# A four-layer model (two scans, two attention and feed-forward layers): TensorE gets zero-weight matmuls, VectorE takes three steps of the last feed-forward stages

## The chip, the cores and the metric

The kernel runs on one core of one Trainium2 chip. The metric is the device time of one execution in microseconds; the median of three runs before the change is 11572.21 us.

## What is computed

The input x is 4 images of 64 x 64 pixels with 96 channels, float32. Four layers follow each other, each with a residual:

```python
# layer 0 and 1: group norm, then a selective scan in four directions (K = 4, 192 channels, 16 states)
xz = x @ in_proj_w.T;  xi, z = split(xz)
xc = silu(depthwise_conv3x3(xi) + conv_b)
xs = four orders of the 4096 pixels of xc
dts, Bs, Cs = split(einsum('bkdl,kcd->bkcl', xs, x_proj_w))
delta = softplus(einsum(dts, dt_w) + dt_b)
h = exp(dt_t * A) * h + (dt_t * u_t) * B_t       # for each pixel t
y = einsum('bkdn,bkn->bkd', h, C_t)
y = layer_norm(sum of the four y + Ds * xs) * silu(z);  x = x + y @ out_proj_w.T
# layer 2 and 3: attention without softmax, then a feed-forward part in 8-bit floats
t = t + attn(layer_norm(t));  t = t + ffn(layer_norm(t))
# ffn: q_mul rounds to e5m2, q_acc to 5 exponent and 10 mantissa bits
h = relu(q_acc(q_acc(q_mul(x) @ q_mul(W1).T) + q_mul(b1)))
y = q_acc(q_acc(q_mul(h) @ q_mul(W2).T) + q_mul(b2))
```

## The kernel before

**Scan phase.** Eight scans (4 images x 2 layers) are run one after another. Each has 16 windows (4 directions x 4 blocks of T = 1024 pixels), so W = 128 windows, and a window has NT = 24 tiles of 128 partitions x 1024 elements: 3072 tiles, numbered n, with i = n % 24. Three groups of GT = 8 tiles make a window. For each tile:
- TensorE broadcasts B into one of two PSUM slots with two bf16 matmuls (`fill`, L1019), after VectorE's scan has released the slot (tile n's after the scan of tile n - 2);
- VectorE multiplies the slot by delta times u (`inp`, L1538) and runs the recurrence (`states`, L1553 and L1549), with the decay that ScalarE has made with an exponential (L1288);
- GpSimd multiplies the states by C (`product`, L1632), and TensorE adds up the states of two tiles in the bank YB with four matmuls in four column strips (`reduce2`, L1032, issued at even i for tiles n - 4 and n - 3). The sum over a group of eight tiles is open from i % 8 = 4 to the reduce2 at i % 8 = 2 of the next group; ScalarE then collects it from YB (L1303).

The last two tiles of a group (`on_pool`) have no fill: ScalarE writes their decay into the slot, and GpSimd makes their input (L1646).

**Side jobs.** Beside the tiles each engine steps through the same list of jobs, two ticks per tile, in an order that the program fixes: "pre" (group norm, and the convolution as nine fp32 matmuls per half and chunk, L826, and L830), "post" (y is loaded and summed with fp32 matmuls, L861, then layer norm L872, L873, L880, projection L887), and "attn" (attention L914 to L952, then the feed-forward part). Per scan there are one pre, one post and, for each image pair, attention jobs. In between TensorE prepares the next windows (L994, L1000, L1010). On every engine instructions run in the order of the program text; a wait holds up all that stands behind it on that engine.

**After the last scan** the jobs of the last window list run alone (`overlapped` is False): post of scan 7 and attn 6 and 7. Chunks of 512 pixels go through three lanes of buffers, FF_LANES = 6 ticks apart. In the feed-forward part chunk c is, at s = tick - 6c: centred on TensorE (s = 0, L961); copied and squared on ScalarE (1, L1204, L1205); its variance on TensorE (2, L965); logarithm and exponential on ScalarE (3, L1208, L1210); scaled and cast by VectorE to `xq` (5, L1527); w1 on TensorE in three parts (6 to 8, L973), each rounded to f16 by ScalarE (7 to 9, L1214); then `s == 10` on ScalarE: three rectifiers with bias (L1218) and the cast to fp8 (L1222); w2 on TensorE (12, L980); rounding (L1226) and bias (L1228) on ScalarE (13); addition to the image on GpSimd (15, L1613). The same functions, with `overlapped` True, serve the feed-forward parts beside the scans, 12 ticks apart and with one lane. Semaphores `fh_a`, `fc_a` and `fb_a` count rectifiers, casts and biases.

Of the kernel before, what the change touches and what calls it, by code (L numbers as in the profile page):

```python
# [13 lines left out]
CH = 96  # L14
# [184 lines left out]
SUMS = (1, 3, 0, 2, K)  # L199
SUM_AT = (0, 2, 4, 8, 10)  # L200
A1_EVERY, A2_EVERY, FF_EVERY = 9, 1, 12
LANES = 3
POST_LANES, A1_LANES, FF_LANES = 13, 4, 6

# [34 lines left out]
def build_program(nc, a, out):  # L239
# [17 lines left out]
    with ctx:  # L257
# [52 lines left out]

        selb = sb("selb", [CH, NQ, 128], BF16)
        neg = sb("neg", [CH, 2, CH], BF16)
        red = sb("red", [128, DB])
        eye = sb("eye", [CH, CH])
        cen = sb("cen", [CH, CH])
# [78 lines left out]
        def rows(v):  # L394
# [51 lines left out]
        mid_p, mid_v = sem("mid_p"), sem("mid_v")  # L446
        ao_p, ao_v = sem("ao_p"), sem("ao_v")
        fc_p, fs_a, fv_p, fr_a, fq_v = sem("fc_p"), sem("fs_a"), sem("fv_p"), sem("fr_a"), sem("fq_v")
        f1_p, f1_a, fh_a, fc_a, f2_p, fy_a, fb_a, fx_g = (sem("f1_p"), sem("f1_a"), sem("fh_a"), sem("fc_a"),
                                                         sem("f2_p"), sem("fy_a"), sem("fb_a"), sem("fx_g"))  # L450
        o_out = sem("o_out")

        after_wait_p, after_wait_v, after_wait_a = sem("after_wait_p"), sem("after_wait_v"), sem("after_wait_a")
# [331 lines left out]
        def _(pe):  # L785
# [106 lines left out]
            def attn(N, overlapped):  # L892
# [61 lines left out]
                for tick in range(ff_ticks(overlapped)):  # L954
                    for c in range(C8):
                        s, m = tick - ff_every(overlapped) * c, M + c
                        v = lane(c, overlapped)
                        if s == 0:
                            pe.wait_ge(ao_v, M + C8)
                            after(pe, f1_a, HT * through(m, c, overlapped))  # L960
                            pe.matmul(ps[0:CH, v.bank, :], cen96[:, :], chunk(c), start=True, stop=True).then_inc(fc_p, 1)  # L961
                        if s == 2:
                            pe.wait_ge(fs_a, m + 1)
                            after(pe, fy_a, through(m, c, overlapped))
                            pe.matmul(ps[0:CH, v.bank + 1, :], o96[:, :], v.sq, start=True, stop=True).then_inc(fv_p, 1)  # L965
                        if s in (6, 7, 8):
                            r = s - 6
                            if r == 0:
                                pe.wait_ge(fq_v, m + 1)
                            if r == 2:  # L970
                                pe.wait_ge(f1_a, HT * m + 1)
                            pe.sem_inc(after_wait_p, 1)
                            pe.matmul(ps[:, v.bank + r % 2, :], w1q[:, l, r * 128:(r + 1) * 128], v.xq,  # L973
                                      start=True, stop=True).then_inc(f1_p, 1)
                        if s == 12:
                            pe.wait_ge(fc_a, m + 1)
                            pe.wait_ge(f1_a, HT * m + 2)
                            pe.sem_inc(after_wait_p, 1)
                            for r in range(HT):
                                mm = pe.matmul(ps[0:CH, v.bank + 1, :], w2q[:, l, r, :], v.hq[:, r, :],  # L980
                                               start=(r == 0), stop=(r == HT - 1))
                            mm.then_inc(f2_p, 1)
                    yield

            stages = {"pre": pre, "post": post, "attn": attn}


            def x_dbl(hf, w):
                s, k = w // STEPS, w % STEPS // NCH
# [23 lines left out]
            def fill(n):  # L1013
                w, i = divmod(n, NT)
                if i == 0:
                    pe.wait_ge(s_a, 6 * w + 6)
                after(pe, scan_v, n - RS + 1)
                for hf in range(2):
                    mm = pe.matmul(ps[:, SLOT + 2 * (n % RS) + hf, :], selb[:, i % GT // 2, :],  # L1019
                                   sbc[:, w % 2, B * hf:B * (hf + 1)], start=True, stop=True)  # L1020
                mm.then_inc(fill_p, 1)

            def reduce2(m):
# [40 lines left out]
            for w in range(W):  # L1064
                if w % STEPS == 0:
                    side = beside(plan[w // STEPS + 1], stages, True)
                    if w == 0:
                        side = follow(head, side)
                if w % STEPS == STEPS - 1:
                    run(side)  # L1070
                for i in range(NT):
                    n = w * NT + i
                    if n + 1 < W * NT and not on_pool(n + 1):
                        fill(n + 1)
                    if i % 2 == 0 and n >= 4:
                        reduce2((n - 4) // 2)
                    for tick in (2 * i, 2 * i + 1):
                        prepare_at(tick, w + 1)
                        prepare_at(tick - 2 * NT, w + 2)
                        next(side, None)  # L1080
            for m in range(W * NP - 2, W * NP):
                reduce2(m)
            run(beside(plan[NSC + 1], stages, False))
# [3 lines left out]
        def _(act):  # L1087
# [78 lines left out]
            def attn(N, overlapped):  # L1166
# [29 lines left out]
                for tick in range(ff_ticks(overlapped)):  # L1196
                    for c in range(C8):
# [13 lines left out]
                        if s in (7, 8, 9):  # L1211
                            r = s - 7
                            act.wait_ge(f1_p, HT * m + r + 1)
                            act.activation(v.h16[:, r, :], ps[:, v.bank + r % 2, :], ACT.Identity).then_inc(f1_a, 1)  # L1214
                        if s == 10:
                            for r in range(HT):
                                act.wait_ge(f1_a, HT * m + r + 1)
                                act.activation(v.h16[:, r, :], v.h16[:, r, :], ACT.Relu, bias=b1q[:, l, r:r + 1]).then_inc(fh_a, 1)  # L1218
                            act.wait_ge(fh_a, HT * (m + 1))
                            after(act, f2_p, through(m, c, overlapped))  # L1220
                            act.sem_inc(after_wait_a, 1)
                            act.activation(v.hq, v.h16, ACT.Identity, saturate=False).then_inc(fc_a, 1)  # L1222
                        if s == 13:
                            act.wait_ge(f2_p, m + 1)
                            after(act, fx_g, through(m, c, overlapped))
                            act.activation(v.y16, ps[0:CH, v.bank + 1, :], ACT.Identity).then_inc(fy_a, 1)  # L1226
                            act.wait_ge(fy_a, m + 1)
                            act.activation(v.y16, v.y16, ACT.Identity, bias=b2q[:, l:l + 1]).then_inc(fb_a, 1)  # L1228
                    yield

            stages = {"pre": pre, "post": post, "attn": attn}
# [139 lines left out]
        def _(dve):  # L1371
# [99 lines left out]
            def attn(N, overlapped):  # L1471
# [47 lines left out]
                for tick in range(ff_ticks(overlapped)):  # L1519
                    for c in range(C8):  # L1520
                        s, m = tick - ff_every(overlapped) * c, M + c
                        v = lane(c, overlapped)
                        if s == 5:
                            dve.wait_ge(fr_a, 2 * m + 2)
                            after(dve, f1_p, HT * through(m, c, overlapped))
                            dve.sem_inc(after_wait_v, 1)
                            dve.tensor_tensor(v.xq, v.xa, ps[0:CH, v.bank + 1, :], ALU.mult, saturate=False).then_inc(fq_v, 1)  # L1527
                    yield

            stages = {"pre": pre, "post": post, "attn": attn}  # L1530
# [45 lines left out]
        def _(pool):  # L1576
            pool.memset(xb[:, :, :], 0.0).then_inc(set_g, 1)
            pool.memset(eps[:, :], 1e-5)
            pool.memset(zero[:, :], 0.0).then_inc(set_g, 1)
            pool.wait_ge(set_v, SET_V)  # L1580

# [19 lines left out]
            def attn(N, overlapped):  # L1601
# [7 lines left out]
                for tick in range(ff_ticks(overlapped)):  # L1609
                    for c in range(C8):  # L1610
                        if tick - ff_every(overlapped) * c == 15:
                            pool.wait_ge(fb_a, M + c + 1)
                            pool.tensor_tensor(chunk(c), chunk(c), rows(lane(c, overlapped).y16), ALU.add).then_inc(fx_g, 1)  # L1613
                    yield

# [137 lines left out]
```

## Time and profile before

| | |
|---|---|
| median of three runs | 11572.21 us (11567.04 to 11578.72) |
| profiled execution | 11564.55 us |
| its span, first to last instruction | 11562.8 us |
| mean granted TensorE clock | 0.741 |
| busy: VectorE, GpSimd, TensorE, ScalarE | 10132.7, 9737.8, 8819.7, 7059.3 us |

All times are microseconds on the one core. PE is TensorE, PEld its weight loads, DVE VectorE, ACT ScalarE, POOL GpSimd. A granted clock of 1.00 is 2.4 GHz, 0.50 is 1.2 GHz; a mean between them is a mixture of the two in time. A group's row gives the count and total busy time, the mean ns of one, then the idle time of the engine just before them and what ended it. A timeline row gives start, duration, engine, line, operation and count of merged instructions, and in brackets the idle time before. An fp32 matmul appears as two records.

### The profile page before, as it was taken

How to read it: one execution, taken by the hardware profiler on the slowest of the kernel's cores; microseconds unless marked ns; L12 is line 12 of the kernel's file. 1: busy time of each engine (PE TensorE's matmuls, PEld its weight loads, DVE VectorE, ACT ScalarE, POOL GpSimd, SP SyncE). 2: the span in 40 equal slices, each digit the busy share in tenths (PEclk: the TensorE clock that was granted, in tenths of full speed). 3: DMA queues.
4: the chain of work that ended last, by engine and by line, in shares of the span. 5: the costliest groups of instructions: out<-in, count | busy, mean ns of one | idle time of the engine just before them, and what ended most of it. 6: DMA issues, size and time to landing. Idle time of an engine off the chain costs nothing.

```text
span 11562.8 us, 94504 instructions
## 1 busy us (share of the span) xinstructions
PE 8819.7 (76%) x26272; PEld 2210.7 (19%) x26272; DVE 10132.7 (88%) x6006; ACT 7059.3 (61%) x10794; POOL 9737.8 (84%) x4231
## 2 busy tenths in 40 slices
PE   6876678876879677769777787787787977777756
PEld 2211111211112111212112121122111221121212
DVE  3899998999889998989989999899989999898871
ACT  4665555665556555667555765566655666567646
POOL 3899988899888998989988888888888889898850
PEclk8875577875779667769777787788677976777766
DMA  3666689566775556656766668957677656565540
GB/s 100 143 139 132 142 150 162 143 138 142 159 160 144 139 145 156 153 130 147 166 150 152 133 141 171 157 133 154 130 159 161 144 133 159 151 149 126 130 118 6
DMA packets 1781802, 1631.74 MB, mean 141 GB/s; under 512 B 1323982, under 2 KB 1325296, under 8 KB 1781276
## 3 DMA queue, kind: packets, MB, share of 16 engines
q1 hardware_dynamic: 1781276, 1625.69, 63.7%
q8 instruction: 212, 3.47, 0.1%
q14 instruction: 314, 2.57, 0.1%
HBM read 625.58 MB, written 194.51 MB: 71 GB/s over the span
## 4 chain that ended last, share of the span: by engine, by line
DVE 16%; PE 16%; issue 15%; POOL 12%; ACT 7%; DMA 3%; SPq 3%; DVEq 0%; POOLq 0%; ACTq 0%
POOL pr L1632 8%; DVE hs L1553 7%; DVE ps L1538 6%; DVE hs L1549 3%; PE ps L1032 3%; PE ps L861 2%; PE ps L1019 2%; PE ps L826 1%; PE ps L1010 1%; ACT dec L1288 1%; POOL bup L1646 1%; POOL dur L1646 1%; PE ps L994 1%; POOL us L1623 1%; SPq L720 1%
## 5 line engine op out<-in xcount | busy, mean ns | idle before, releaser
L1632 POOL TENSOR_TENSOR pr<-hs,crep 128x1024 f32<-128x1024 f32 x3072 | 7183.5, 2354 | 1194.5 <-PE ps L1032 571.8
L1553 DVE TENSOR_TENSOR_SCAN hs<-dec,carry,ps 128x1024 f32<-128x1024 f32 x1728 | 4054.7, 2346 | 240.4 <-POOL pr L1632 14.0
L1538 DVE TENSOR_TENSOR ps<-ps,dur 128x1024 f32<-128x1024 f32 x2304 | 2790.1, 1211 | 513.9 <-PE ps L1019 372.5
L1019 PE MATMUL ps<-sbc,selb 96*128 96x512 bf16 x4608 | 1844.5, 493 | 1789.8 <-DVE hs L1553 1248.3
L1288 ACT ACTIVATE dec<-dtr,ac 128x1024 f32<-128x1024 f32 x2304 | 2610.9, 1136 | 436.4 <-DVE hs L1553 427.7
L1032 PE MATMUL ps<-pr,red 128*32 128x512 f32 x12288 | 2285.0, 827 | 33.0 <-POOL pr L1632 24.5
L1295 ACT ACTIVATE carry<-hs 128x1 f32<-128x1 f32 x2304 | 456.9, 199 | 2434.7 <-DVE hs L1553 2265.4
L1553 DVE TENSOR_TENSOR_SCAN hs<-dec,zero,ps 128x1024 f32<-128x1024 f32 x576 | 1351.5, 2346 | 86.0 <-ACT dec L1288 14.1
L826 PE MATMUL ps<-xb,tapw 96*96 96x512 f32 x2304 | 1187.2, 637 | 55.9 <-ACT sd L1122 53.4
L1019 PEld LDWEIGHTS ps<-sbc,selb 96*128 96x128 bf16 x4608 | 382.5, 108 | 3922.6 <-DVE hs L1553 2313.5
L1288 ACT ACTIVATE ps<-dtr,ac 128x1024 f32<-128x1024 f32 x768 | 848.4, 1105 | 400.0 <-DVE hs L1553 399.8
L1646 POOL TENSOR_TENSOR dur<-dur,brep 128x1024 f32<-128x1024 f32 x384 | 907.1, 2362 | 46.2 <-DVE ps L1538 46.1
L1646 POOL TENSOR_TENSOR bup<-dur,brep 128x1024 f32<-128x1024 f32 x384 | 905.0, 2357 | 27.3 <-DMA brep<-bc_d 27.3
L1010 PE MATMUL ps<-xdf,tapw 6*96 6x512 f32 x1024 | 781.0, 852 | 45.7 <-ACT de L1263 29.1
L994 PE MATMUL ps<-us,xp 96*102 96x512 f32 x1024 | 685.7, 806 | 78.9 <-ACT us L1241 59.5
L1623 POOL TENSOR_TENSOR us<-us,de 96x1024 f32<-96x1024 f32 x256 | 602.4, 2353 | 157.1 <-ACT de L1272 157.1
L861 PE MATMUL ps<-sd,eye 96*96 96x512 f32 x896 | 644.1, 840 | 105.1 <-DMA sd<-y_d 102.1
L1549 DVE TENSOR_TENSOR_SCAN hs<-ps,carry,bup 128x1024 f32<-128x1024 f32 x288 | 671.3, 2331 | 57.9 <-ACT ps L1288 44.1
L1549 DVE TENSOR_TENSOR_SCAN hs<-ps,carry,dur 128x1024 f32<-128x1024 f32 x288 | 670.4, 2328 | 17.7 <-POOL dur L1646 9.5
L826 PEld LDWEIGHTS ps<-xb,tapw 96*96 96x96 f32 x2304 | 359.4, 170 | 775.3 <-issue 680.1
L1032 PEld LDWEIGHTS ps<-pr,red 128*32 128x32 f32 x12288 | 276.5, 124 | 1175.8 <-issue 887.5
L1255 ACT ACTIVATE sbc<-ps 96x512 bf16<-96x512 f32 x768 | 444.0, 578 | 25.9 <-PE ps L1000 25.6
(224 smaller groups left out, 7595.9 us busy)
## 6 DMA issues: line engine op xcount, KB each, us to landing
dtr<-de SPq DMA_DIRECT2D x768, 512.0 KB, 8.0
dur<-us SPq DMA_DIRECT2D x768, 512.0 KB, 8.6
crep<-bc_d SPq DMA_DIRECT2D x512, 512.0 KB, 6.6
ust<-u_d SPq DMA_DIRECT2D x256, 384.0 KB, 5.9
y_d<-yst SPq DMA_DIRECT2D x768, 128.0 KB, 3.3
sd<-y_d SPq DMA_DIRECT2D x448, 192.0 KB, 5.1
brep<-bc_d SPq DMA_DIRECT2D x128, 512.0 KB, 5.6
u_d<-sd SPq DMA_DIRECT2D x64, 384.0 KB, 3.2
```

The lines of the kernel that those rows point to most:

```text
L826: mm = pe.matmul(bank, tap[:, t, h * CH:(h + 1) * CH], xb[:, c * ROWS + t // 3:c * ROWS + t // 3 + ROWS, t % 3:t % 3 + SIDE], start=(t == ...
L861: mm = pe.matmul(ps[0:CH, bank + h, :], eye[:, :] if k < K else dg[:, l, h, :], v, start=(i == 0), stop=(i == K))
L994: mm = pe.matmul(ps[0:XROWS, PB, :], xp[:, l, h, k, :], us[:, half(h, w), B * hf:B * (hf + 1)], start=(h == 0), stop=(h == 1))
L1010: pe.matmul(ps[0:CH, PB, :], dtw[:, order[s][1], k, h * CH:(h + 1) * CH], xdf[XD:XROWS, :], start=True, stop=True, tile_position=(XD, 0)). ...
L1019: mm = pe.matmul(ps[:, SLOT + 2 * (n % RS) + hf, :], selb[:, i % GT // 2, :], sbc[:, w % 2, B * hf:B * (hf + 1)], start=True, stop=True)
L1032: mm = pe.matmul(ps[32 * strip:32 * strip + 32, YB, :], red[:, :], pr[:, (2 * m + j) % RP, B * hf:B * (hf + 1)], start=(q == 0), stop=(q = ...
L1288: act.activation(to, dtr[:, 2 * (G % 2) + i % 2, :], ACT.Exp, scale=ac[:, order[s][1], k, i:i + 1]).then_inc(exp_a, 1)
L1538: dve.tensor_tensor(slot(n), slot(n), dur[:, 2 * (G % 2) + i % 2, :], ALU.mult).then_inc(bu_v, 1)
L1549: dve.tensor_tensor_scan(hs[:, n % RH, :], slot(n), bup[:, :] if i % 2 else dur[:, 2 * (G % 2), :], init, ALU.mult, ALU.add).then_inc(scan ...
L1553: dve.tensor_tensor_scan(hs[:, n % RH, :], dec[:, others(n) % RD, :], slot(n), init, ALU.mult, ALU.add).then_inc(scan_v, 1)
L1632: pool.tensor_tensor(pr[:, n % RP, :], hs[:, n % RH, :], crep[:, q, :], ALU.mult).then_inc(prod_g, 1)
L1646: pool.tensor_tensor(to, v, brep[:, :], ALU.mult).then_inc(bup_g, 1)
```

## The change

First, in the scan phase, `keep_busy()` issues BUSY = 3 matmuls at the end of tile i on TensorE, for the tiles in which the sum in YB is open (i % 8 not 2 or 3). Their weights are `nil`, 96 x 128 zeros in bf16, their moving data 512 columns of `selb`, and they add zero to YB. In the tiles after i % 8 = 2 and 3 the two fill matmuls are issued twice instead. Second, in the feed-forward parts after the last scan, VectorE does the three rectifiers (s = 8, 9, 10), the cast (11) and the second bias (14) instead of ScalarE. Semaphores are renamed; the feed-forward parts beside the scans stay on ScalarE.

```diff
@@ TensorE
+            def open_sum(i):
+                return i % GT not in (2, 3)
+            def keep_busy():
+                for _ in range(BUSY):
+                    pe.matmul(ps[:, YB, :], nil[:, :], selb[:, :, :].rearrange("p q n -> p (q n)"),
+                              start=False, stop=False, skip_group_check=True)
@@ fill(n)
-                for hf in range(2):
-                    mm = pe.matmul(ps[:, SLOT + 2 * (n % RS) + hf, :], selb[:, i % GT // 2, :],
-                                   sbc[:, w % 2, B * hf:B * (hf + 1)], start=True, stop=True)
+                for again in range(1 if open_sum(i - 1) else 2):
+                    for hf in range(2):
+                        mm = pe.matmul(ps[:, SLOT + 2 * (n % RS) + hf, :], selb[:, i % GT // 2, :],
+                                       sbc[:, w % 2, B * hf:B * (hf + 1)], start=True, stop=True)
                 mm.then_inc(fill_p, 1)
@@ end of a tile on TensorE
                         next(side, None)
+                    if n >= 4 and open_sum(i):
+                        keep_busy()
@@ ScalarE, feed-forward
-                        if s == 10:
+                        if overlapped and s == 10:
...
                             act.activation(v.y16, ps[0:CH, v.bank + 1, :], ACT.Identity).then_inc(fy_a, 1)
-                            act.wait_ge(fy_a, m + 1)
-                            act.activation(v.y16, v.y16, ACT.Identity, bias=b2q[:, l:l + 1]).then_inc(fb_a, 1)
+                            if overlapped:
+                                act.wait_ge(fy_a, m + 1)
+                                act.activation(v.y16, v.y16, ACT.Identity, bias=b2q[:, l:l + 1]).then_inc(f_bias, 1)
@@ VectorE, feed-forward
+                        if not overlapped and s in (8, 9, 10):
+                            r = s - 8
+                            dve.wait_ge(f1_a, HT * m + r + 1)
+                            dve.tensor_scalar(v.h16[:, r, :], v.h16[:, r, :], b1q[:, l, r:r + 1], 0.0,
+                                              ALU.add, ALU.max).then_inc(f_relu, 1)
+                        if not overlapped and s == 11:
+                            dve.wait_ge(f_relu, HT * (m + 1))
+                            after(dve, f2_p, through(m, c, overlapped))
+                            dve.tensor_copy(v.hq, v.h16, saturate=False).then_inc(f_cast, 1)
+                        if not overlapped and s == 14:
+                            dve.wait_ge(fy_a, m + 1)
+                            dve.tensor_scalar(v.y16, v.y16, b2q[:, l:l + 1], None, ALU.add).then_inc(f_bias, 1)
@@ GpSimd, at the start
+            pool.memset(nil[:, :], 0.0)
```

## Rows read from the trace of the kernel before

**Rows 1.** The page: busy time of the engines, and TensorE's clock in 40 slices.

```profile
PE 8819.7 (76%) x26272; PEld 2210.7 (19%) x26272; DVE 10132.7 (88%) x6006; ACT 7059.3 (61%) x10794; POOL 9737.8 (84%) x4231
...
PEclk8875577875779667769777787788677976777766
```

**Rows 2.** Windows, busy us and instructions by engine, then clock, DMA, GB/s.

```profile
800.00:1400.00 600.00, 406.80 (x1164) 69.34 (x1164) 581.58 (x322) 333.10 (x483) 566.89 (x246) 0.57 0.62 130
...
652.16:678.12 25.96, 24.59 (x86) 7.66 (x84) 25.00 (x15) 18.79 (x30) 22.68 (x11) 1.00 0.54 124
...
sum 2070.00, PE 1882.49 PEld 547.00 DVE 1898.62 ACT 1450.84 POOL 1836.21; mean PE 268.93 PEld 78.14 DVE 271.23 ACT 207.26 POOL 262.32
...
1500.00:2100.00 600.00, 482.71 (x1337) 109.27 (x1336) 537.95 (x314) 344.30 (x507) 527.32 (x228) 0.75 0.85 157
...
sum 4070.00, PE 3220.07 PEld 747.89 DVE 3687.45 ACT 2364.44 POOL 3613.69; mean PE 460.01 PEld 106.84 DVE 526.78 ACT 337.78 POOL 516.24
...
11460.00:11560.00 100.00, 49.88 (x89) 14.00 (x88) 9.39 (x14) 67.45 (x104) 8.91 (x8) 0.61 0.07 14
```

**Rows 3.** Timeline of VectorE, no side job: start us, us, what.

```profile
811.53 1.21 DVE L1538 TENSOR_TENSOR ps<-ps,dur 128x1024 f32<-128x1024 f32 x1
...
837.64 1.21 DVE L1538 TENSOR_TENSOR ps<-ps,dur 128x1024 f32<-128x1024 f32 x1
```

**Rows 4.** Timeline of TensorE beside the convolution, 650 to 700.

```profile
652.16 0.59 PE L1019 MATMUL ps<-sbc,selb 96*128 96x512 bf16 x2
652.59 1.88 PE L994 MATMUL ps<-us,xp 96*102 96x512 f32 x4
```

**Rows 5.** Waits of VectorE in the whole span: total, times, longest.

```profile
DVE ps L1538 <- PE ps L1019: 372.5, 241, 7.3
```

**Rows 6.** Windows around three waits of VectorE for the fill.

```profile
410.54:413.85 3.31, 3.27 (x5) 0.60 (x3) 2.87 (x2) 2.01 (x4) 2.05 (x2) 0.50 0.28 64
...
1834.50:1844.83 10.33, 8.48 (x20) 2.36 (x21) 3.00 (x2) 3.23 (x5) 7.66 (x5) 0.60 1.02 286
...
11023.33:11028.50 5.17, 4.05 (x12) 1.41 (x15) 2.86 (x2) 4.24 (x7) 1.97 (x1) 0.54 0.01 3
```

**Rows 7.** Timeline of the longest of them, in the first post.

```profile
1836.35 3.73 PE L861 MATMUL ps<-sd,eye 96*96 96x512 f32 x4 [5.66 <-DMA sd<-y_d]
...
1844.83 1.23 DVE L1538 TENSOR_TENSOR ps<-ps,dur 128x1024 f32<-128x1024 f32 x1 [7.34 <-PE ps L1019]
```

**Rows 8.** Timeline of the last two feed-forward stages.

```profile
11358.53 0.72 ACT L1228 ACTIVATE crep<-crep,b2q 96x512 f16<-96x512 f16 x1
...
11363.22 0.66 ACT L1208 ACTIVATE ps<-ps,eps 96x512 f32<-96x512 f32 x1 [1.14 <-PE ps L965]
...
11364.40 1.93 ACT L1218 ACTIVATE sd<-sd,b1q 128x512 f16<-128x512 f16 x3
...
11364.66 0.68 DVE L1527 TENSOR_TENSOR pr<-pr,ps 96x512 fp8e5<-96x512 f32 x1 [11.04 <-ACT ps L1210]
...
11366.47 1.48 ACT L1222 ACTIVATE sd<-sd 128x1536 fp8e5<-128x1536 f16 x1
...
11369.38 0.63 PE L973 MATMUL ps<-pr,w1q 96*128 96x512 fp8e5 x1
11369.80 1.92 PE L961 MATMUL ps<-xb,cen 96*96 96x512 f32 x2
...
11372.89 2.02 PE L965 MATMUL ps<-crep,o 96*96 96x512 f32 x2 [0.31 <-ACT crep L1205]
...
11479.99 1.48 PE L980 MATMUL ps<-sd,w2q 128*96 128x512 fp8e5 x3 [4.92 <-ACT sd L1222]
...
11555.78 1.48 PE L980 MATMUL ps<-pr,w2q 128*96 128x512 fp8e5 x3 [4.23 <-ACT pr L1222]
```

**Rows 9.** Groups of VectorE in the first 60 us, casts to fp8.

```profile
L1376 DVE CAST w1q<-dur 96x768 fp8e5<-96x768 f32 x1 | 0.5, 549 | 0.0
L1377 DVE CAST w2q<-dur 128x576 fp8e5<-128x576 f32 x1 | 0.4, 449 | 0.0
```

More of the change, by code:

```diff
@@ L201 @@
 A1_EVERY, A2_EVERY, FF_EVERY = 9, 1, 12
+BUSY = 3
 LANES = 3
@@ L312, in build_program @@
         neg = sb("neg", [CH, 2, CH], BF16)
+        nil = sb("nil", [CH, 128], BF16)
         red = sb("red", [128, DB])
@@ L448, in build_program @@
         fc_p, fs_a, fv_p, fr_a, fq_v = sem("fc_p"), sem("fs_a"), sem("fv_p"), sem("fr_a"), sem("fq_v")
-        f1_p, f1_a, fh_a, fc_a, f2_p, fy_a, fb_a, fx_g = (sem("f1_p"), sem("f1_a"), sem("fh_a"), sem("fc_a"),
-                                                         sem("f2_p"), sem("fy_a"), sem("fb_a"), sem("fx_g"))
+        f1_p, f1_a, f_relu, f_cast, f2_p, fy_a, f_bias, fx_g = (sem("f1_p"), sem("f1_a"), sem("f_relu"), sem("f_cast"),
+                                                               sem("f2_p"), sem("fy_a"), sem("f_bias"), sem("fx_g"))
         o_out = sem("o_out")
@@ L975, in attn @@
                         if s == 12:
-                            pe.wait_ge(fc_a, m + 1)
+                            pe.wait_ge(f_cast, m + 1)
                             pe.wait_ge(f1_a, HT * m + 2)
@@ L1214, in attn @@
                             act.activation(v.h16[:, r, :], ps[:, v.bank + r % 2, :], ACT.Identity).then_inc(f1_a, 1)
-                        if s == 10:
+                        if overlapped and s == 10:
                             for r in range(HT):
                                 act.wait_ge(f1_a, HT * m + r + 1)
-                                act.activation(v.h16[:, r, :], v.h16[:, r, :], ACT.Relu, bias=b1q[:, l, r:r + 1]).then_inc(fh_a, 1)
-                            act.wait_ge(fh_a, HT * (m + 1))
+                                act.activation(v.h16[:, r, :], v.h16[:, r, :], ACT.Relu, bias=b1q[:, l, r:r + 1]).then_inc(f_relu, 1)
+                            act.wait_ge(f_relu, HT * (m + 1))
                             after(act, f2_p, through(m, c, overlapped))
                             act.sem_inc(after_wait_a, 1)
-                            act.activation(v.hq, v.h16, ACT.Identity, saturate=False).then_inc(fc_a, 1)
+                            act.activation(v.hq, v.h16, ACT.Identity, saturate=False).then_inc(f_cast, 1)
                         if s == 13:
@@ L1611, in attn @@
                         if tick - ff_every(overlapped) * c == 15:
[L1612 removed]
+                            pool.wait_ge(f_bias, M + c + 1)
                             pool.tensor_tensor(chunk(c), chunk(c), rows(lane(c, overlapped).y16), ALU.add).then_inc(fx_g, 1)
```

## The prediction

> **What bounds the kernel now.** I read the page's busy shares first, then the windows stage by stage, then the waits of VectorE, and last the timelines of the two places that the change touches. Over the whole span VectorE is the busiest engine at 88%, GpSimd has 84% and TensorE 76%, and TensorE's granted clock is a mixture of its two levels: the slices of PEclk run from 5 to 8 tenths [rows 1]. The windows show why [rows 2]. The scan phase goes through 3072 tiles with side jobs beside them.
> - With no side job (800 to 1400) VectorE is busy for 581.58 of 600 us, or 97%. Records of neighbours touch there, so 97% is its ceiling. Eight tiles go from 811.53 to 837.64 [rows 3], 26.11 us, or 3.264 us a tile. TensorE is busy 68% at clock 0.57, mostly on its level of 1.2 GHz, and nobody waits for it.
> - Beside the convolution of "pre" (seven stretches, 2070 us together) VectorE falls to 1898.62/2070 = 91.7% and TensorE is at 91%, with a clock of 1.00 in eight tiles without a disturbance (652.16 to 678.12). A tile takes 3.264 x 0.969/0.917 = 3.45 us, which makes 600 tiles.
> - Beside "post" (seven stretches, 4070 us) VectorE has 90.6%, TensorE 79%; the first stretch, 1500 to 2100, has clock 0.75.
> - After the last scan, in the two feed-forward stages, VectorE does next to nothing (9.39 of 100 us), ScalarE is busy for 67% and TensorE for half, at clock 0.61.
>
> What VectorE waits for in the scan phase is above all the broadcast of B, L1019: 372.5 us in 241 waits [rows 5]. I looked at the granted clock in the 3 us before each of these waits and during it: of the 223 waits over 0.3 us (369 us), 151 with 279 us stand at a mean clock under 0.75; the first and the last of them are [rows 6]. So up to 279 us of the scan phase go with a slow TensorE clock.
>
> **Part 1, the zero-weight matmuls.** In six of eight tiles TensorE gets 3 more 512-column bf16 matmuls, and in the other two the 2 fill matmuls are issued twice: 18 + 4 = 22 in eight tiles, 8448 in all. The matmuls go into bank YB; the sums of L1032 there and ScalarE's collecting keep their order, so no engine but TensorE gets a wait from them. Their price is the spacing of such matmuls in a full queue. At clock 1.00 the two fills of 652.16 are followed by the next group at 652.59 [rows 4]: 0.215 us each. At the low level the w1 matmul of 11369.38 is followed by the next group at 11369.80 [rows 8], 0.42 us; I take twice 0.215, 0.43 us each. So 22 cost 4.73 us per eight tiles at the high level, 0.59 us a tile, and 1.18 us at the low one.
>
> Beside the convolution this lands on an engine that is full. The eight tiles from 652.16 to 678.12 take 25.96 us with TensorE busy for 24.59 [rows 2] at clock 1.00. With 4.73 more it needs 29.32 us, more than VectorE's 26.11: TensorE becomes the bound there, at 3.665 us a tile. Against 3.45 now that is +0.215 us on 600 tiles, **+129 us**. The low end is 3.55 us a tile, if the records' gaps between short matmuls absorb part of the addition (+60 us); the high end is 3.80, if waits of the kind seen today (TensorE 91% busy, not 100%) stay on top (+210 us). I take the middle, since a queue that never runs dry has few of them.
>
> Of the Trainium skill one rule bears on that price. Its page "TensorE: Matmul & The Clock Gate", section "Back-to-back issue gap", gives some 131 ns per matmul for a sustained stream of weight loads and 512-column matmuls. By that figure eight tiles would take 24.59 + 2.9 = 27.5 us, 3.44 a tile, and the term would be an estimated 0 in place of the cost above. The trace's 0.215 us [rows 4] disagrees and is used.
>
> Everywhere else the added matmuls lie in time in which TensorE waits. With no side job VectorE has 2.35 us of scan and 1.21 us of multiply between the release of a slot and the need for the next fill, and the fill itself needs 0.43 to 1.0; 3 zero matmuls (0.65 to 1.3 us) fit. There they bring nothing either, as VectorE is at its ceiling. I put 0 on these 2100 us, with +20 as the bad end, since at the low level TensorE would need about 68% of 3.264 plus 1.18, 3.4 us a tile, until the clock rises.
>
> What comes back is a part of the 279 us. It can't be all. The program order of TensorE is fixed: a zero matmul that stands behind a blocked instruction runs after it, not instead of the idle time. The worst wait shows it [rows 7]: TensorE sits idle for 5.66 us on a load of y, then works off its backlog, and VectorE gets its fill 7.34 us late at 1844.83. The first rows of that backlog run at the low level (four passes in 3.73 us, against 1.88 for four passes in [rows 4]). Nothing in the change fills those 5.66 us; it adds two sets of three matmuls, 1.3 to 2.6 us, to the backlog. The smaller waits, which come after ordinary idle time between fills, should shrink by half or more. I take 45% of 279, **-126 us**, between 5% (-15) and 85% (-240). Attention, whose matmuls wait for ScalarE and VectorE step by step, gives perhaps 12 us more, **-12 us** (0 to -40).
>
> What I leave aside is the idle time itself: the window around that wait has clock 0.60 [rows 6], it begins with the late load, and no added matmul makes the load come sooner.
>
> **Part 2, the last two feed-forward stages.** There a chunk goes round a loop in which ScalarE has everything. The w2 matmuls of neighbouring chunks start at 11479.99 and, seven chunks on, at 11555.78: 10.83 us a period [rows 8]. In a period ScalarE does the evacuations, logarithm and exponential (11363.22), three rectifiers (11364.40, 1.93 us), the cast (11366.47, 1.48 us), only then w2 starts (it waits for L1222 as in the row of 11555.78), and the y16 bias follows (11358.53, 0.72 us). The change takes 1.93 + 1.48 + 0.72 us from ScalarE. VectorE then has, per chunk, three 128x512 f16 ops, a cast of 1536 columns and a 512-column add. Neither exists in the trace. Bounds from casts [rows 9]: 768 columns took 0.549 us and 576 took 0.449, so 0.52 ns a column, and 1536 columns take 0.95 us; 512 take 0.42. The other end is one column in 1.04 ns: 1.75 and 0.68 (the 512-column op of L1527 has 0.68, [rows 8]). In all 2.6 to 4.5 us a period, beside ScalarE, so VectorE doesn't become the bound.
>
> What is late next is the normalisation loop: w1 of chunk D at 11369.38, centring of E, its squares, o96 at 11372.89 for 2.02 us, 0.03 to the logarithm: 5.56 us; then from the logarithm at 11363.22 to the end of xq at 11364.66 + 0.68: 2.12 us; then w1 of E. That is 7.7 us at the low level [rows 8]. The matmuls in it shorten at the high level by up to 1.9 us, so 5.8 to 7.7. The clock was 0.61 there [rows 2], so I take 7.4. Fourteen periods save 14 x (10.83 - 7.4) = 48 us, and the last chunk of each stage has a shorter way to its end: 3.41 us of rectifiers and cast become 0.42 + 0.95, and the bias saves 0.3, some 2.3 us, twice. Together **-53 us** (-40 if VectorE runs at one column per 1.04 ns, with its cast in the loop; -75 if the clock rises). The wait order is safe: on VectorE only the xq of the next chunk is queued behind the cast, and it needs the exponential, which ends later than the cast. GpSimd's adds wait for the bias as before and have slack.
>
> **The sum.** +129 - 126 - 12 - 53 = -62 us against the profiled execution's 11564.55 us; the median of the runs, 11572.21, lies 7.7 above it. So 11564.6 - 62 + 7.7 = **11510 us**.
>
> **The rivals.**
> - *A: the clock stays up nearly everywhere.* Six zero matmuls in a pause keep TensorE at 2.4 GHz between fills, the small waits go, attention follows: -240 - 40 in the scan phase, +110 beside the convolution, -75 at the end, in sum -245, so 11327; halfway to the forecast it gives 11410. For it: where TensorE's queue is full, its clock is 1.00 [rows 2]. Against: [rows 7], and that TensorE at the high level with the added work is busy for under two thirds of a stretch with no side job. Chance 0.18, time about 11400.
> - *E: a full queue takes the added matmuls for less than their spacing*, since weight loads and short records overlap. Then eight tiles beside the convolution stay within today's 3.45 us a tile, the +129 falls away and 11381 is left. Against it: the 0.215 us of [rows 4] are read in just such a full queue. The Trainium skill's figure above is the reason to list it. Chance 0.05.
> - *B: the convolution loses more than the rest gives.* One mechanism: beside "pre" TensorE is already full, and 22 more matmuls per eight tiles are paid in full, at 3.80 us a tile (+210), while only 15% of the waits come back (-42) and the end gives -50. Sum +118, so 11690. It decides against the change from the point where the scan phase loses over 76 us, since the end gives 53 and 23 is the measurable bound. For it: 24.59 of 25.96 us busy. Chance 0.20, times from 11595 to 11700.
> - *C: both halves cancel.* The scan phase loses 30 to 76 us and the end gives it back. Chance 0.14, 11549 to 11595.
> - *D: the change does not do what it says*: the clock stays near 0.57 beside nothing and the added matmuls run at 0.43 us. Then the stretches without side jobs slow from 3.264 to 3.4 us a tile, 4% of 2100 us, +84 us on top of B. It is part of B's chance, 0.03 of it.
>
> **How the numbers follow.** Forecast (11450 to 11549) 0.43, A 0.18, E 0.05, C 0.14, B with D 0.20. A measurement can tell about 0.2%, 23 us, from no change. Faster: 0.43 + 0.18 + 0.05 = 0.66; same 0.14; slower 0.20. For eight in ten I leave out the far half of A and the far half of B: 11370 to 11625.
>
> **What would show it.** In the changed profile: the PEclk slices up from 5 to 8 tenths; beside the convolution TensorE at 97% or more and VectorE at 86 to 89%, a tile at 3.6 to 3.7 us; beside "post" VectorE at 92 to 93%; waits for L1019's successor beside "post" (now most of 372.5 us) down by half with the ones behind y loads still there; with no side job 97% as now. In the end the w2 matmuls 7.0 to 7.8 us apart and ScalarE waiting between. The forecast is wrong if the added matmuls cost much less than 0.215 us each in a full queue, if the clock beside "post" stays at 0.75, or if the loop at the end is set by VectorE's cast.

## The result: 1.6% slower

| | before | after |
|---|---|---|
| median | 11574.33 us | 11752.85 us (11744.01 to 11767.27) |
| ratio | | 1.0157, 95% interval 1.0142 to 1.0173 |
| span of the profiled execution | 11562.8 us | 11749.7 us |
| from the start of the first scan to that of the last | 10942.7 us | 11174.4 us |
| from there to the end | 430.4 us | 385.4 us |
| mean granted clock | 0.741 | 0.852 |

The clock rose as the change meant it to, the end became 45 us shorter, and the scan phase became 232 us longer. The page of the changed kernel, to be read against [rows 1]:

```profile
PE 9950.4 (85%) x34714; PEld 2931.7 (25%) x34714; DVE 10189.4 (87%) x6086; ACT 7003.7 (60%) x10714; POOL 9746.2 (83%) x4232
PEclk8887788887889778879888898899888988888876
```

TensorE went from 76% to 85% busy and its slices from 5 to 8 tenths up to 6 to 9. VectorE has the same scans and multiplies as before in a longer span. I numbered the scans in both traces (3072 of them) and compared equal pieces of work. The windows below hold the convolution's matmuls of seven scans (first sum), and the sums over y of seven posts (second sum). The same pieces before took 1919 us with TensorE busy for 1778 and VectorE for 1752 (clock 0.93 to 0.96), and 3620 us with 2902 and 3252 (clock 0.75 to 0.78). The last row is 600 us with no side job, to be read against the first of [rows 2].

```profile
2184.00:2474.00 290.00, 286.17 (x1037) 95.23 (x1036) 252.72 (x139) 184.65 (x261) 242.93 (x105) 0.99 0.60 138
sum 2036.00, PE 2011.43 PEld 668.71 DVE 1773.64 ACT 1332.31 POOL 1707.87; mean PE 287.35 PEld 95.53 DVE 253.38 ACT 190.33 POOL 243.98
...
1559.00:2100.00 541.00, 481.04 (x1563) 131.84 (x1562) 467.36 (x272) 300.09 (x437) 458.61 (x198) 0.85 0.86 159
sum 3682.00, PE 3250.41 PEld 913.01 DVE 3264.17 ACT 2091.31 POOL 3205.09; mean PE 464.35 PEld 130.43 DVE 466.31 ACT 298.76 POOL 457.87
...
800.00:1400.00 600.00, 457.56 (x1674) 109.05 (x1672) 580.92 (x323) 329.85 (x479) 567.49 (x245) 0.79 0.64 138
```

- Beside the convolution TensorE is now busy for 286.17 of 290 us at clock 0.99, and for 2011.43 of 2036 us, or 99%, in the seven windows together (before: 1778 of 1919, or 93%). It is the bound: +117 us for the same work.
- Beside post the clock went from 0.75 to 0.85, and the same work takes 62 us more, not less.
- With no side job VectorE has 580.92 us where it had 581.58, at clock 0.79 in place of 0.57. That higher clock bought nothing there. A VectorE scan takes 2346 ns in both traces, so VectorE's own work did not get slower; it waits more.

By groups of eight tiles, each put down to the side job that has matmuls in it, the 232 us are: beside the convolution +123 (3.494 to 3.691 us a tile), post +51, feed-forward +26, attention +5, none of these +27.

The waits grew where TensorE is waited for. The first row answers [rows 5] (372.5 us in 241 waits); GpSimd's wait for a free product buffer had 571.8 us before.

```profile
DVE ps L1568 <- PE ps L1034: 569.8, 384, 9.7
...
POOL pr L1663 <- PE ps L1047: 829.9, 384, 8.6
```

Sorted by the mean granted clock of each wait and the 3 us before it (waits over 0.3 us), as in the prediction:

| mean clock | before | after |
|---|---|---|
| under 0.75 | 279 us in 151 | 262 us in 111 |
| 0.75 to 0.95 | 63 us in 41 | 82 us in 30 |
| 0.95 and over | 27 us in 31 | 201 us in 136 |

The waits with a slow clock are nearly all still there, and a new class stands beside them: waits at a full clock, for a TensorE with too much in its queue.

The traces also show what TensorE did before each of these waits ended. I added up its records between the release of the slot (the end of the scan two tiles before) and VectorE's late start. In the changed kernel, zero-weight matmuls stand there in 249 of the 277 waits (491 of 545 us) and take 288 us of TensorE's time. In the waits with a clock under 0.75, TensorE's idle time fell from 123 us before to 67 after, but zero-weight matmuls take 133 us in its place. Most of the increase is at one place: VectorE's waits for the first tile of a group went from 177 to 320 us, all others together from 192 to 225.

At the end, the loop of the feed-forward stages, timeline rows that answer [rows 8], and a window over the second stage:

```profile
11582.19 0.96 DVE L1554 CAST crep<-crep 128x1536 fp8e5<-128x1536 f16 x1
...
11585.45 0.35 DVE L1557 TENSOR_SCALAR crep<-crep,b2q 96x512 f16<-96x512 f16 x1 [0.42 <-ACT crep L1243]
...
11583.30 1.48 PE L982 MATMUL ps<-crep,w2q 128*96 128x512 fp8e5 x3 [0.43 <-DVE crep L1554]
11585.17 0.59 PE L975 MATMUL ps<-sd,w1q 96*128 96x512 fp8e5 x1 [0.39 <-DVE sd L1545]
...
11588.63 2.02 PE L967 MATMUL ps<-pr,o 96*96 96x512 f32 x2 [0.31 <-ACT pr L1222]
11591.08 1.49 PE L982 MATMUL ps<-sd,w2q 128*96 128x512 fp8e5 x3 [0.43 <-DVE sd L1554]
...
11688.00:11744.00 56.00, 45.88 (x71) 12.09 (x71) 25.48 (x45) 31.26 (x56) 7.80 (x7) 0.50 0.12 25
```

The cast takes 0.96 us on VectorE and the bias 0.35; w2 starts every 7.78 us in place of 10.83. TensorE is busy for 45.88 of 56 us in that stage and its clock is 0.50 throughout; it idles 0.43, 0.39 and 0.31 us in a period.

### The profile page after: what moved, and what is told of

Same layout as the page of the kernel before. It is cut to its first block, busy times and chain, and to the rows that moved or that the text cites. A ratio compares the mean times of both kernels' runs of the same rounds, so it can differ in the third digit from the quotient of the medians.

```text
span 11749.7 us, 111386 instructions
## 1 busy us (share of the span) xinstructions
PE 9950.4 (85%) x34714; PEld 2931.7 (25%) x34714; DVE 10189.4 (87%) x6086; ACT 7003.7 (60%) x10714; POOL 9746.2 (83%) x4232
## 4 chain that ended last, share of the span: by engine, by line
PE 37%; issue 18%; DVE 17%; POOL 15%; ACT 7%; DMA 3%; SPq 3%; DVEq 0%; POOLq 0%; ACTq 0%
POOL pr L1663 10%; PE ps L828 7%; DVE hs L1583 7%; DVE ps L1568 6%; PE ps L1047 6%; PE ps L999 5%; PE ps L1034 5%; PE ps L863 3%; DVE hs L1579 3%; PE ps L1024 3%; PE ps L1008 2%; POOL bup L1677 1%; POOL us L1654 1%; ACT dec L1306 1%; POOL dur L1677 1%
## 5 line engine op out<-in xcount | busy, mean ns | idle before, releaser
L1663 POOL TENSOR_TENSOR pr<-hs,crep 128x1024 f32<-128x1024 f32 x3072 | 7193.5, 2356 | 1428.6 <-PE ps L1047 829.9
L1583 DVE TENSOR_TENSOR_SCAN hs<-dec,carry,ps 128x1024 f32<-128x1024 f32 x1728 | 4054.2, 2346 | 234.9 <-POOL pr L1663 10.4
L1568 DVE TENSOR_TENSOR ps<-ps,dur 128x1024 f32<-128x1024 f32 x2304 | 2792.8, 1212 | 707.9 <-PE ps L1034 569.8
L1034 PE MATMUL ps<-sbc,selb 96*128 96x512 bf16 x6144 | 1989.9, 432 | 1146.1 <-DVE hs L1583 918.0
L999 PE MATMUL ps<-selb,nil 96*128 96x512 bf16 x6906 | 2148.0, 426 | 0.0
L1047 PE MATMUL ps<-pr,red 128*32 128x512 f32 x12288 | 1994.4, 727 | 13.8 <-POOL pr L1663 11.5
L1583 DVE TENSOR_TENSOR_SCAN hs<-dec,zero,ps 128x1024 f32<-128x1024 f32 x576 | 1351.3, 2346 | 83.8 <-ACT dec L1306 12.8
L1034 PEld LDWEIGHTS ps<-sbc,selb 96*128 96x128 bf16 x6144 | 564.7, 105 | 2547.2 <-DVE hs L1583 1500.4
L999 PEld LDWEIGHTS ps<-selb,nil 96*128 96x128 bf16 x6906 | 671.1, 106 | 2063.1 <-issue 1783.1
L828 PE MATMUL ps<-xb,tapw 96*96 96x512 f32 x2304 | 1136.5, 613 | 20.3 <-ACT sd L1139 17.9
L1024 PE MATMUL ps<-xdf,tapw 6*96 6x512 f32 x1024 | 659.1, 727 | 34.9 <-ACT sbc L1273 20.6
L863 PE MATMUL ps<-sd,eye 96*96 96x512 f32 x896 | 597.9, 785 | 62.4 <-DMA sd<-y_d 60.1
L1008 PE MATMUL ps<-us,xp 96*102 96x512 f32 x1024 | 595.3, 712 | 57.9 <-ACT us L1259 48.5
```

The source lines that it names most:

```text
L828: mm = pe.matmul(bank, tap[:, t, h * CH:(h + 1) * CH], xb[:, c * ROWS + t // 3:c * ROWS + t // 3 + ROWS, t % 3:t % 3 + SIDE], start=(t == ...
L863: mm = pe.matmul(ps[0:CH, bank + h, :], eye[:, :] if k < K else dg[:, l, h, :], v, start=(i == 0), stop=(i == K))
L999: pe.matmul(ps[:, YB, :], nil[:, :], selb[:, :, :].rearrange("p q n -> p (q n)"), start=False, stop=False, skip_group_check=True)
L1024: pe.matmul(ps[0:CH, PB, :], dtw[:, order[s][1], k, h * CH:(h + 1) * CH], xdf[XD:XROWS, :], start=True, stop=True, tile_position=(XD, 0)). ...
L1047: mm = pe.matmul(ps[32 * strip:32 * strip + 32, YB, :], red[:, :], pr[:, (2 * m + j) % RP, B * hf:B * (hf + 1)], start=(q == 0), stop=(q = ...
L1568: dve.tensor_tensor(slot(n), slot(n), dur[:, 2 * (G % 2) + i % 2, :], ALU.mult).then_inc(bu_v, 1)
```

## The experiments

All of these kernels keep VectorE's share at the end. "Scan" is the difference in the time from the first to the last scan in one profiled execution, "end" that of the time behind it. One profile of a kernel lies up to 30 us beside its median (e3; 17 us in e5, under 12 in the others), so the difference of medians (each against the kernel before in the same session) is given too; less the -57.5 us of e1 it is a second estimate of the scan phase's part. The expectations below were written with slightly other spans (10932 us before, +235 after, +99 in e4); counted from the first to the last scan these are 10942.7, +232 and +102.

| run | added matmuls | median | scan | end | clock |
|---|---|---|---|---|---|
| after | 22 in 8 tiles | +178.5 | +232 | -45 | 0.852 |
| e1_tail_only | none | -57.5 | -4 | -51 | 0.741 |
| e2_zero_no_refill | 18 | +146.4 | +191 | -44 | 0.830 |
| e3_refill_only | 4 | -66.1 | +16 | -43 | 0.769 |
| e4_not_beside_pre | 22, not beside pre | +46.9 | +102 | -45 | 0.838 |
| e5_short | 18 of 64 columns, not beside pre | -27.4 | +35 | -46 | 0.746 |
| e6_six | 36, not beside pre | +242.1 | +288 | -53 | 0.875 |
| e7_gap | 18 in two tiles, not beside pre | +357.7 | +418 | -56 | 0.797 |
| e9_not_before_first_fill | 15, not beside pre | +48.0 | +88 | -43 | 0.807 |
| e10_only_before_first_fill | 3, not beside pre | -23.8 | +43 | -52 | 0.749 |
| e8_tail_zero | none in the scans, 3 a chunk at the end | -68.1 | -3 | -66 | 0.743 |
| e11_tail_zero_two | the same, 6 a chunk | -69.5 | +5 | -71 | 0.745 |

**The two halves apart.** Edit of e1_tail_only, relative to the changed kernel (e2 and e3 have one of the two hunks each):

```diff
-                for again in range(1 if open_sum(i - 1) else 2):
+                for again in range(1):
...
-                    if n >= 4 and open_sum(i):
-                        keep_busy()
```

> Only VectorE's share in the last two feed-forward stages; no zero-weight matmuls and no second fills. My theory (the end gives some 45 us, the scan phase is where all of the loss lies, and beside the convolution it is TensorE's queue): scan phase as before, 10932 us from the first to the last scan, the part after it 385 us in place of 430, total 11520 to 11530, ratio 0.996. Rival (the tail gains less, because something of the scan phase lends it a warmer clock): the part after the last scan stays over 400 us, total over 11535.

Measured: 11517.78 us, ratio 0.9957 (0.9942 to 0.9971). The scan phase is back at 10939 us, the end is 51 us shorter (379 us, under the 385 expected). So all of the loss is in the added matmuls, and VectorE's share alone is a gain.

> The changed kernel with its three zero-weight matmuls, but each fill issued once. Theory Q (queue time: what counts is TensorE time added, wherever it stands): 18 of the 22 added matmuls of eight tiles stay, so about 18/22 of the loss stays in the scan phase: +190 of +235 us over the kernel before, total near 11707. Rival R (the second fills are the harm, since each stands before the increment that VectorE waits for, 0.43 to 0.86 us, while the zero matmuls stand behind it): the loss falls by more than half, to under +110 us, total under 11630.

> The changed kernel with the second fills in two of eight tiles, but without the zero-weight matmuls. Theory Q: 4/22 of the loss, +40 us in the scan phase, total near 11560. Rival R (second fills are the harm): over +120 us in the scan phase, total over 11640. If neither part alone adds up to the whole, they work on each other through the clock.

Measured: 11721.74 us (ratio 1.013, 1.0103 to 1.0157) and 11509.2 us (0.9946, 0.9931 to 0.996). The second fills alone cost at most 16 us by e3's profile and nothing by its median, less than the 40 that theory Q had for them; the zero-weight matmuls carry the loss, as Q had it (+191 us for +190). Rival R falls. Beside the convolution e2 has +79 us and e3 -14: TensorE had a little room there, and the last four of 22 matmuls then cost the other 44. Beside post e2 has +80 us with fewer matmuls than the changed kernel, which has +51; with one profile of each, the parts of a scan phase are known to some 30 us only.

**The convolution left out.** The changed kernel remembers which side job it steps through:

```diff
             for kind, n in jobs:
+                beside_kind[0] = kind
                 yield from stages[kind](n, overlapped)
+            beside_kind[0] = None
...
-                    if n >= 4 and open_sum(i):
+                    if n >= 4 and open_sum(i) and (beside_kind[0] != "pre"):
```

The second fills have the same condition.

> The changed kernel without its added matmuls in the tiles that run beside the side job pre (group norm and convolution). The step of the prediction that held by the traces (TensorE full beside the convolution, 3.49 us a tile to 3.69, +128 us) says that these 128 us go and nothing else does: scan phase +105 us over before, total 11620 to 11640. Rival: the loss beside the convolution comes from what the other stages leave behind, and under 60 us of it go, total over 11690.

Measured: 11622.26 us, ratio 1.0045 (1.0032 to 1.0058). Beside the convolution the pace is 3.483 us a tile (3.494 before, 3.691 after), and 130 us of the loss are gone. What remains, +102 us by the trace and +104 by the medians, is what the prediction had put at -138.

**Time or instructions, three or six.** e5 and e6 start from e4, with each fill once:

```diff
-                    pe.matmul(ps[:, YB, :], nil[:, :], selb[:, :, :].rearrange("p q n -> p (q n)"),
+                    pe.matmul(ps[:, YB, 0:64], nil[:, :], selb[:, 0, 0:64],        # e5_short
...
-BUSY = 3
+BUSY = 6                                                                          # e6_six
```

> As the run without added matmuls beside pre (+99 us in the scan phase), each fill issued once, and the zero-weight matmuls cut from 512 to 64 columns: the same 18 instructions in eight tiles, but hardly any TensorE time. Theory Q (what is lost outside the convolution is TensorE time that stands in front of a late fill): the scan phase returns to within 20 us of the kernel before, total 11500 to 11540. Rival I (the instructions themselves, their weight loads and decoding, cost): over +60 us stay.

> Not beside pre, each fill once, but six zero-weight matmuls of 512 columns at the end of a tile in place of three. Theory Q: twice the TensorE time, so the loss outside pre at least doubles, from about +85 to +170 us or more over the kernel before in the scan phase, total over 11690. Rival C (the clock: three are too few to hold 2.4 GHz, six would hold it and take the slow bursts away): mean clock over 0.90, waits of VectorE for the fill beside post fall under those before, and the scan phase is faster than with three.

Measured: 11537.36 us (0.9971, 0.9956 to 0.9986) and 11806.77 us (1.0212, 1.0192 to 1.0233). The groups of the zero-weight matmuls and VectorE's waits for the fill, e5 first:

```profile
L1003 PE MATMUL ps<-selb,nil 96*128 96x64 bf16 x5370 | 532.3, 216 | 0.0
...
DVE ps L1572 <- PE ps L1038: 410.7, 239, 7.9
...
L1003 PE MATMUL ps<-selb,nil 96*128 96x512 bf16 x10740 | 2854.3, 406 | 0.0
...
DVE ps L1572 <- PE ps L1038: 660.0, 362, 10.7
```

With 64 columns the same number of instructions costs 30 us by the medians and 35 by the trace, and the waits for the fill are 411 us. That lies between the bounds of the two theories (under 20, over 60): most of the loss goes with the columns, and what is left may be the 532 us of TensorE time that the short ones still take, or the instructions themselves. With 10740 long ones the waits are 660 us, and post alone loses 215 us. The clock is 0.875, the highest of all runs, and the kernel is among the slowest. Rival C (too few to hold the clock) asked for over 0.90, which six don't reach; 292 us of waits in 89 still stand at a clock under 0.75, and those at a full clock are 331 us. More matmuls gave more clock and less speed. Doubling the zero-weight matmuls, and leaving out the second fills, nearly triples the loss against e4 (104 to 300 us by the medians).

**Where they stand.** e7 puts nine each behind tiles 5 and 6, where I thought that no fill follows for two tiles; e9 and e10 split the places of three between all but tile 6 and tile 6 alone:

```diff
-                    if n >= 4 and open_sum(i):
+                    if n >= 4 and i % GT in (5, 6) and beside_kind[0] != "pre":               # e7_gap, BUSY = 9
+                    if n >= 4 and i % GT in (0, 1, 4, 5, 7) and beside_kind[0] != "pre":      # e9
+                    if n >= 4 and i % GT in (6,) and beside_kind[0] != "pre":                 # e10
```

> Not beside pre, each fill once; the 18 zero-weight matmuls of eight tiles all stand at the ends of tiles 5 and 6 of a group, nine at each, where the next two tiles have no fill, so that most of their time passes before VectorE needs TensorE again. Theory Q with place: the same number of matmuls costs under a third of the +85 us, or even gives up to 30 us back through the warmer clock. Rival N (number counts, not place): the scan phase stays at +70 us or more.

Measured: 11922.4 us, ratio 1.0312 (1.0292 to 1.0333), the slowest of all, where I had expected the cheapest. The timeline shows the mistake:

```profile
999.69 4.02 PE L1003 MATMUL ps<-selb,nil 96*128 96x512 bf16 x9
1003.64 1.68 PE L1051 MATMUL ps<-pr,red 128*32 128x512 f32 x8
1005.25 2.12 PE L1003 MATMUL ps<-selb,nil 96*128 96x512 bf16 x9
1007.21 0.59 PE L1038 MATMUL ps<-sbc,selb 96*128 96x512 bf16 x2
...
1005.51 4.67 POOL L1667 TENSOR_TENSOR pr<-hs,crep 128x1024 f32<-128x1024 f32 x2 [1.00 <-PE ps L1051]
...
1007.91 1.23 DVE L1572 TENSOR_TENSOR ps<-ps,dur 128x1024 f32<-128x1024 f32 x1 [1.36 <-PE ps L1038]
```

The nine behind tile 5 run at the low clock (4.02 us) in front of the reduction, which GpSimd needs for its buffers (it waits 1.00 us); the nine behind tile 6 (2.12 us at the full clock) stand in front of the fill for the next group's first tile. VectorE waits 1.36 us for that fill. TensorE has no fill to make at the starts of tiles 5 and 6, but the program issues the next one at the start of tile 7, and the reduction between is on GpSimd's way. The pause was not free time. Rival N's bound is met but not its reason: 18 matmuls at two places cost four times what e4's 22 cost, so place does count.

> Not beside pre, each fill once, three zero-weight matmuls at the ends of the tiles with i % 8 in (0, 1, 4, 5, 7): all places but the one of tile 6, where they stand between the reduction that waits for GpSimd and the fill for the first tile of the next group. Theory F (most of the loss outside pre is at that one fill: nine matmuls a place there cost +674 us of waiting): the scan phase is at most 40 us over the kernel before, although 15 of 18 matmuls stay. If the warmer clock gives anything at all, it shows here, as a scan phase under that of the kernel before. Rival (loss goes by number): 15/18 of the loss of about 110 us stays, +90 us.

> The other half: the three zero-weight matmuls at the end of tile 6 of each group alone, not beside pre, each fill once. Theory F: +60 to +110 us in the scan phase with a sixth of the matmuls. Rival (number): +18 us.

Measured: 11618.63 us (1.0051, 1.0034 to 1.0068) and 11546.8 us (0.9978, 0.9967 to 0.9988). By the medians 15 matmuls cost +106 us and 3 cost +34; by number the rival had said +90 and +18, and theory F at most +40 and at least +60. The traces say +88 and +43. So theory F falls in the main: the other places cost too. It also rested on a figure read wrongly, since 672 us are all of e7's waits for the first fill of a group, of which 177 us are there in the kernel before. How dear a single place is these runs don't settle: 15 and 3 make 140 us by the medians when added up, but e4, which has both and the second fills, has 104; and the intervals of e10 and of e1 (0.9942 to 0.9971) overlap. In e9's scan phase the place in front of the first fill is free of added matmuls, and still nothing comes back from a clock of 0.807. Beside post it loses 77 us, and its waits with a mean clock under 0.75 are 326 us in 141, more than in the kernel before.

**At the end.** e8 takes e1 and adds one zero-weight matmul in front of and behind o96 and one behind w2, for chunks after the last scan (with a wait that YB has been collected):

```diff
+                            if not overlapped:
+                                keep_busy()
                             pe.wait_ge(fs_a, m + 1)
                             after(pe, fy_a, through(m, c, overlapped))
                             pe.matmul(ps[0:CH, v.bank + 1, :], o96[:, :], v.sq, start=True, stop=True).then_inc(fv_p, 1)
+                            if not overlapped:
+                                keep_busy()
...
                             mm.then_inc(f2_p, 1)
+                            if not overlapped:
+                                keep_busy()
...
-BUSY = 3
+BUSY = 1
```

> VectorE's share at the end alone (11517.78 us), plus one zero-weight matmul at three places of each chunk in the last two feed-forward stages, where TensorE idles 0.31, 0.43 and 0.39 us in a period of 7.78 us at clock 0.5. Theory K (TensorE's clock follows how full it is, and it is 80% busy there): the clock rises to over 0.8 in these stages, the period falls from 7.78 to 6.0 to 6.8 us, total 15 to 25 us under the run without them. Rival: the clock stays at 0.5 and each added matmul of 0.43 us that doesn't fit the idle time adds up, 14 periods of +0.2 to 0.4 us, 3 to 6 us slower.

Measured: 11496.65 us, ratio 0.9948 (0.9932 to 0.9965). Its intervals overlap with those of e1, so the medians alone don't separate the two; the traces do. The second feed-forward stage in e1 and in e8, as windows, then two starts of w2 in e8:

```profile
11455.00:11500.00 45.00, 37.29 (x58) 9.47 (x56) 20.51 (x37) 25.84 (x46) 6.70 (x6) 0.50 0.10 23
...
11445.00:11490.00 45.00, 31.88 (x91) 10.35 (x89) 26.56 (x43) 30.35 (x55) 7.80 (x7) 0.91 0.15 31
...
11459.02 0.82 PE L987 MATMUL ps<-crep,w2q 128*96 128x512 fp8e5 x3 [1.13 <-DVE crep L1559]
11464.83 0.82 PE L987 MATMUL ps<-sd,w2q 128*96 128x512 fp8e5 x3 [1.13 <-DVE sd L1559]
```

The clock is 0.91 in place of 0.50 in these windows, and the end is 66 us shorter than before, not 51. Four of the six full periods of that stage last 5.81 us in place of 7.78, the other two 7.4 and 7.7; in the first stage (11330 to 11374) the clock is 0.85 and they last 5.8 to 7.5. At 0.91 most of the stage is at 2.4 GHz; the records cover 31.88 of 45 us there, against 37.29 in e1, which is at 1.2 GHz throughout.

> As the kernel with one zero-weight matmul at three places of each chunk of the last feed-forward stages, with two at each. If the clock is already held at 2.4 GHz with one, the second only adds 0.2 us at places with 1.1 us idle: same time within 10 us, or 5 us faster where the first stage still toggled. If it isn't held, the period grows where the clock is 1.2 GHz and the time rises by 5 to 15 us.

Measured: 11501.09 us, ratio 0.995 (0.9933 to 0.9967). Same as with one within 10 us, as expected. By the traces the clock is held better (1.00 from 11450 to 11491, 0.96 from 11338 to 11374), most periods last 5.94 us in place of 5.8 to 7.7, and the end is 5 us shorter than in e8. Both beat the kernel before and the changed one; e8_tail_zero has the lowest median measured.

## Why the prediction was wrong

The forecast was 11510 us and faster, with 11370 to 11625; measured were 11752.85 us and slower. By its own steps:

- **Beside the convolution: right.** The step said +129 us and 3.665 us a tile, from 22 matmuls of 0.215 us on a TensorE already busy for 24.59 of 25.96 us. The trace shows +117 to +123 us and 3.691 us a tile, and e4 takes 130 us away. By the 131 ns per matmul of the Trainium skill (page "TensorE: Matmul & The Clock Gate", section "Back-to-back issue gap"), the prediction's rival E, there would have been no loss; the trace disagrees: nine zero-weight matmuls are followed by the next group after 1.96 us at a full clock in e7, 0.22 us each.
- **The matmuls hidden elsewhere: wrong.** The step costed them at nothing because three of them fit into the time between a slot's release and the next fill. That compares one queue entry with one gap. TensorE's order also holds the reduction, which waits for GpSimd and on which GpSimd's buffers depend, and the side job's fp32 matmuls; when one of these is late, the zero-weight matmuls behind it stand in front of the fill. The changed kernel's trace has them there in 249 of 277 waits, and e5 against e4 and e6 shows that the loss goes mostly with their length. The groups of eight tiles with none of these jobs, where the step had 0 (+20 at worst), lost 27 us.
- **What comes back: wrong, and the step that turned the sign.** It took 45% of the 279 us of waits at a slow clock as a gain (-126), and 12 us for attention. Those waits fell by 17 us (279 to 262), and those at a full clock rose by 174. Away from the convolution the scan phase lost 109 us where the steps had -138: 247 us of error, all but the whole difference. The clock did rise beside post, from 0.75 to 0.85, which the text had named as the sign that the gain depends on; but VectorE's share of the time there went to 88.7%, not 92 to 93%. The flaw was in the reading: that a wait goes together with a slow clock doesn't say that the clock causes it. The longest one begins with a blocked instruction ([rows 7]): TensorE is idle for 5.66 us and then runs at the low level, and zero-weight matmuls that stand behind that instruction can't fill the idle time. Where they did fill some of it, 56 us less idle time before the slow waits, they took 133 us themselves. The ends of the range, 5% to 85% of the 279 us, had no loss in them at all, though the text itself counted 1.3 to 2.6 us more backlog for the worst wait.
- **The end: right in kind, somewhat too good.** 53 us were forecast, 45 measured (51 in e1, where the scans have no added matmuls). The cast took 0.96 us against 0.95 estimated, a rectifier 0.43 to 0.47 against 0.42, the bias 0.35. The loop has the 7.7 us that the prediction worked out for the low level; I had taken 7.4 from the clock of 0.61 there. In the changed kernel TensorE is busier (82% by its records, half before) and the clock is 0.50.
- **The rivals.** B named the side and half of the mechanism, at 11690 us; its price beside the convolution (+210) was too high and its 42 us from the waits had the wrong sign. A, with a chance of 0.18 (its halfway time is 11418 us, not 11410), needed waits that go away as matmuls are added; in e6, with the highest mean clock, they are 660 us. E, with 0.05, falls with the +123 us beside the convolution.

What stays open is how the loss beside post divides between reductions that come late for GpSimd and fills that come late for VectorE; both waits rose (571.8 to 829.9 and 372.5 to 569.8 us), and each may feed the other. Both instructions stand in TensorE's one program order here, and no run separates them.

## What to carry to other kernels

Work added to an in-order engine "in its idle time" is only free if nothing behind it can be late for another reason; count every wait in that queue, not only the one that the work is put next to, and let the range reach to a loss. A higher granted clock is no gain in itself: ask which wait ends on TensorE while its clock is low, and whether that wait began with idle time that the added work can't fill. Moving a step off the engine that carries a dependence loop is worth what the next loop leaves, and there, with TensorE in the loop and slack at known places, one zero-weight matmul per place did pay, 15 us by the traces.

## What the runs showed of the hardware

TensorE stayed at a granted clock of 0.50 for a whole feed-forward stage while its records cover 45.88 of 56 us, with gaps of 0.31, 0.43 and 0.39 us in a period. In the kernel before, with TensorE busy for 49.88 of 100 us there, the clock was 0.61 ([rows 2]). Three more 512-column bf16 matmuls a chunk, in a loop otherwise unchanged, went with a clock of 0.91 in the window shown. The Trainium skill, page "TensorE: Matmul & The Clock Gate", section "Why this matters for your kernels", advises to keep TensorE busy; the trace agrees in e8, while the stage of the changed kernel is busy by its records and has the low clock all the same. What the chip looks at there these runs don't tell. In the scans the added matmuls raised the clock from 0.57 to 0.79 with no side job, where VectorE's share of the time stayed at 97%.
